# Cross-attention stage: normalising and quantising moved to GpSimd, two fp32 products split into three products of rounded parts, the residual added in the output buffer

## The reference

```python
x2 = (x - mean(x)) / sqrt(var(x) + 1e-5)
q = (x2 @ Wq + bq) / sqrt(32)                  # per head
q = round(q / s) * s                           # s = max|q| / 127, per token and head
attn = softmax(q @ k.T)                        # k, v quantised ahead of this stage
attn = round(attn / a) * a                     # a = max(attn) / 255, per row
x = x + (attn @ v) @ Wp + bp
```

## Time and profile before

| what | value |
|---|---|
| time, median of 3 runs | 3387.66 us (3382.36 to 3388.56) |
| time of the profiled execution | 3388.41 us |
| its span, first to last instruction | 3386.2 us |
| mean granted TensorE clock | 0.978 |
| this stage, from its first VectorE instruction to the start of the last `add` | 1911.38 to 2209.21 us |

### The profile page before, as it was taken

The page is one execution under the profiler, slowest core; times in us unless marked ns, Lnnn a source line. Parts: engine busy times, 40 slices in busy tenths (PEclk is TensorE's granted clock), DMA queues, the critical chain, the costliest instruction groups (busy, mean ns, idle before and its releaser), DMA issues. The chain is left out here.

```text
span 3386.2 us, 59964 instructions
## 1 busy us (share of the span) xinstructions
PE 3173.4 (94%) x18834; PEld 2548.5 (75%) x18834; DVE 2200.1 (65%) x4849; ACT 1902.5 (56%) x4657; POOL 1666.0 (49%) x3107
## 2 busy tenths in 40 slices
PE   6799999999999999999989888879998999998998
PEld 3688888888888888888878555568876777777543
DVE  5577777777777677777753388865548576685432
ACT  3677777777767777777631177743436464463111
POOL 2777787777787777778630000035553002011322
PEclk8899999999999999999989899999999999999999
DMA  4222222222222222222353323433334222221853
GB/s 113 65 73 70 53 74 66 69 73 63 61 69 72 70 63 73 69 59 70 85 175 99 128 106 143 152 110 119 99 112 150 81 66 73 83 75 66 263 101 54
DMA packets 432407, 310.46 MB, mean 92 GB/s; under 512 B 130496, under 2 KB 347456, under 8 KB 431072
## 3 DMA queue, kind: packets, MB, share of 16 engines
q1 hardware_dynamic: 423792, 289.57, 28.9%
q0 software_dynamic: 8432, 18.88, 2.8%
HBM read 177.97 MB, written 130.43 MB: 91 GB/s over the span
## 5 line engine op out<-in xcount | busy, mean ns | idle before, releaser
L631 PE MATMUL gd_PJ<-xn_lead,gd_w_rest 128*128 128x512 f32 x1024 | 420.8, 411 | 0.5 <-DVE gd_w_rest L786 0.5
L631 PE MATMUL gd_PJ<-xn_lead,gd_w_lead 128*128 128x512 f32 x1024 | 402.4, 393 | 0.0
L631 PE MATMUL gd_PJ<-xn_rest,gd_w_lead 128*128 128x512 f32 x1024 | 401.2, 392 | 0.0
L1079 POOL TENSOR_TENSOR gd_prod<-gd_L,gd_T 32x14 f32<-32x14 f32 (+6 forms) x896 | 323.3, 361 | 70.5
L1082 POOL TENSOR_TENSOR gd_T<-gd_T,gd_prod 32x14 f32<-32x14 f32 (+6 forms) x896 | 313.4, 350 | 71.7 <-POOL gd_prod L1079 2.7
L793 DVE SCALAR_TENSOR_TENSOR gd_conv<-gd_pre,gd_cur_a,gd_conv 128x512 f32<-128x512 f32 x384 | 301.8, 786 | 12.8 <-ACT gd_conv L958 2.4
L631 PEld LDWEIGHTS gd_PJ<-xn_lead,gd_w_lead 128*128 128x128 f32 x1024 | 193.2, 189 | 43.4
L631 PEld LDWEIGHTS gd_PJ<-xn_lead,gd_w_rest 128*128 128x128 f32 x1024 | 194.0, 189 | 38.4 <-DVE gd_w_rest L786 0.9
L631 PEld LDWEIGHTS gd_PJ<-xn_rest,gd_w_lead 128*128 128x128 f32 x1024 | 194.4, 190 | 35.2
L932 DVE SCALAR_TENSOR_TENSOR gd_og<-gd_B,ptab,gd_gate 128x512 f32<-128x512 f32 x64 | 48.0, 751 | 243.6 <-PE gd_B L645 243.6
L640 PE MATMUL gd_B<-gd_W,gd_Lo 128*128 128x64 f32 (+1 forms) x1536 | 174.6, 257 | 23.8 <-DMA gd_T<-inverse_image 14.7
(11 more groups left out here) (476 smaller groups left out, 8744.3 us busy)
## 6 DMA issues: line engine op xcount, KB each, us to landing
expert_rows<-xt_blank SPq DMA_DIRECT2D x16, 2112.0 KB, 7.3
turned_queries_keys<-f_wq SPq DMA_DIRECT2D x16, 1280.0 KB, 6.0
x_wo<-decay_sums SPq DMA_DIRECT2D x64, 256.0 KB, 3.8
triangles<-gd_Lo SPq DMA_DIRECT2D x64, 256.0 KB, 3.5
gd_W<-turned_image SPq DMA_DIRECT2D x64, 256.0 KB
gd_T<-inverse_image SPq DMA_DIRECT2D x64, 256.0 KB
gated_outputs<-gd_og SPq DMA_DIRECT2D x64, 256.0 KB, 2.8
go_ogt<-gated_outputs SPq DMA_DIRECT2D x16, 1024.0 KB, 5.9
```

Source lines behind the costliest of these rows:

```text
L631: mm = pe.matmul(bank, w_parts[wp][:, j, k, :], rhs, start=(k == 0 and wp == 1), stop=(k == KT - 1 and wp + xp == 0))
L1079: nc.gpsimd.tensor_tensor(prod[:, rows, 0:j], L16[:, rows, j:j + 1].to_broadcast(shape), T16[:, j:j + 1, 0:j].to_broadcast(shape), ALU.mul ...
```

## The change

- `queries` and `project` use operands of two rounded parts each (a lead in the 32-bit rounded matmul type, and the rest, value minus lead). Each k-tile takes three matmuls, rest x lead, lead x rest and lead x lead, in place of one fp32 product. ScalarE's copies `copy_xT` and `copy_oT` write the lead, and two new VectorE steps, `rest_x` and `rest_o`, subtract it from PSUM.
- At the start of the stage `wq` (its buffer now lies in `E`) is split by ScalarE (lead) and VectorE (rest), k-tile by k-tile; `wp` is split by GpSimd before it clears `blank`.
- `normalise` for tiles 3 and on moves to GpSimd as two instructions with a broadcast column, and `quantise` for tiles 2 and on as four. VectorE keeps the scale and its reciprocal (`inverse_scale`, now right after `biased`) and copies the scale at the end of the slot (`keep_scale`). Tiles 0 to 2 and 0 to 1 stay on VectorE.
- `fetch` writes the residual plus bias into `y` itself, after it has waited for the store of that buffer; `add` no longer waits for the store.

```diff
-            def fetch(t, par):
-                nc.gpsimd.tensor_tensor(xt[:, par, :], xres[:, bass.ds(t, 1), :]..., bpb[:, :], ALU.add).then_inc(bias_ready, 1)
+            def fetch(t, half, par):
+                pool.wait_ge(out_done[par], half * 16 + 16)
+                nc.gpsimd.tensor_tensor(y[:, par, :], xres[:, bass.ds(t, 1), :]..., bpb[:, :], ALU.add).then_inc(bias_ready, 1)
+            def normalise(t):
+                pool.wait_ge(x_turned, t)
+                nc.gpsimd.tensor_copy(st[:, 0:1], mean[:, bass.ds(t, 1)]).then_inc(st_ready, 1)
+                nc.gpsimd.tensor_copy(st[:, 1:2], rstd[:, bass.ds(t, 1)]).then_inc(st_ready, 1)
+                pool.wait_ge(st_ready, (t - 2) * 2)
+                nc.gpsimd.tensor_tensor(xn[:, :], xres[...], st[:, 0:1].to_broadcast([P, DIM]), ALU.subtract).then_inc(xc_ready, 1)
+                pool.wait_ge(xc_ready, t - 2)
+                nc.gpsimd.tensor_tensor(xn[:, :], xn[:, :], st[:, 1:2].to_broadcast([P, DIM]), ALU.mult).then_inc(xn_ready, 1)
+            def quantise(t):
+                pool.wait_ge(qr_ready, t + 1)
+                nc.gpsimd.tensor_tensor(qf[:], qf[:], bc(qr[:, :], XD), ALU.mult).then_inc(qn_ready, 1)
...
+                nc.gpsimd.tensor_tensor(qf[:], qf[:], scale[...].to_broadcast([P, XH, XD]), ALU.mult).then_inc(qn_ready, 1)
...
+                nc.gpsimd.tensor_tensor(qf[:], qf[:], magic[...].to_broadcast([P, XH, XD]), ALU.add).then_inc(qn_ready, 1)
...
+                nc.gpsimd.tensor_tensor(qi[:, :], qf[...], magic[:, 0:1].to_broadcast([P, DIM]), ALU.subtract).then_inc(qi_ready, 1)
             def slot(t, i, s, left):                       # GpSimd
+                if left > 2:
+                    normalise(t + 3)
+                if left > 1:
+                    quantise(t + 2)
                 if left > 0:
                     pool.wait_ge(y_ready, t + 1)
-                    fetch(t + 1, 1 - s)
+                    fetch(t + 1, i + s, 1 - s)
+            for g in range(GR):                            # GpSimd, ahead of the blank
+                nc.gpsimd.tensor_copy(wp_parts[0][:, g, :], wp[:, g, :]).then_inc(wp_led, 1)
+                pool.wait_ge(wp_led, g + 1)
+                nc.gpsimd.tensor_tensor(wp_parts[1][:, g, :], wp[:, g, :], wp_parts[0][:, g, :].bitcast(F32), ALU.subtract).then_inc(wp_split, 1)
                 for k in ks:                               # TensorE, queries; project alike
-                    mm = pe.matmul(psQ[:, :], xT[:, k, :], wq[:, k, :], ...)
+                    for xp, part in ((1, 0), (0, 1), (0, 0)):
+                        mm = pe.matmul(psQ[:, :], xT[xp][:, k, :], wq_parts[part][:, k, :], ...)
             def slot(t, i, s, left):                       # VectorE
                 integers(t, 0)
+                if left > 1:
+                    rest_x(t + 2)
                 maxima(t, s, 2)
...
                 if left > 1:
                     biased(t + 2)
+                    inverse_scale(t + 2)
                 integers(t, 2)
+                if prev:
+                    rest_o(t - 1)
                 if left > 0:
                     maxima(t + 1, 1 - s, 0)
                 copy_p(t, 2)
-                if left > 2:
-                    normalise(t + 3)
...
                 if left > 1:
-                    quantise(t + 2, s)
+                    keep_scale(s)
                 if prev:
-                    add(t - 1, i - 1 + s, 1 - s)
+                    add(t - 1, 1 - s)
+            for k in range(KT):                            # VectorE, start of the stage, after normalise(1)
+                dve.wait_ge(wq_led, k + 1)
+                nc.vector.tensor_tensor(wq_parts[1][:, k, :], wq[:, k, :], wq_parts[0][:, k, :].bitcast(F32), ALU.subtract).then_inc(wq_split, 1)
+                if k == 0:
+                    rest_x(0)
+            rest_x(1)
```

More of the change, by code:

```diff
@@ L1448, in cross_tiles @@
         o = sb("o", [P, XH, XD])
-        oT = sb("oT", [P, GR, P])
+        oT = [sb(n, [P, GR, P], F32R) for n in ("oT_lead", "oT_rest")]
         y = sb("y", [P, 2, DIM])
+        magic, scale = sb("magic", [P, 1]), sb("scale", [P, 1])
         blank = sb("blank", [P, ROW])
@@ new lines, in quantise @@
+            def quantise(t):
+                pool.wait_ge(qr_ready, t + 1)
+                nc.gpsimd.tensor_tensor(qf[:], qf[:], bc(qr[:, :], XD), ALU.mult).then_inc(qn_ready, 1)
+                pool.wait_ge(qn_ready, (t - 2) * 3 + 1)
+                nc.gpsimd.tensor_tensor(qf[:], qf[:], scale[:, 0:1].unsqueeze(2).to_broadcast([P, XH, XD]), ALU.mult).then_inc(qn_ready, 1)
+                pool.wait_ge(qn_ready, (t - 2) * 3 + 2)
+                nc.gpsimd.tensor_tensor(qf[:], qf[:], magic[:, 0:1].unsqueeze(2).to_broadcast([P, XH, XD]), ALU.add).then_inc(qn_ready, 1)
+                pool.wait_ge(qn_ready, (t - 2) * 3 + 3)
+                nc.gpsimd.tensor_tensor(qi[:, :], qf[:].rearrange("p h d -> p (h d)"), magic[:, 0:1].to_broadcast([P, DIM]), ALU.subtract).then_inc(qi_ready, 1)
@@ L1534, in queries @@
                 for k in ks:
-                    mm = pe.matmul(psQ[:, :], xT[:, k, :], wq[:, k, :], start=(k == 0), stop=(k == KT - 1))
+                    for xp, part in ((1, 0), (0, 1), (0, 0)):
+                        mm = pe.matmul(psQ[:, :], xT[xp][:, k, :], wq_parts[part][:, k, :],
+                                       start=(k == 0 and xp == 1), stop=(k == KT - 1 and xp + part == 0))
                 if ks[-1] == KT - 1:
@@ L1577, in project @@
                     pe.wait_ge(oT_ready, t + 1)
+                    if isinstance(t, int) and t == 0:
+                        pe.wait_ge(wp_split, GR)
                 for g in gs:
-                    mm = pe.matmul(psQ[:, :], oT[:, g, :], wp[:, g, :], start=(g == 0), stop=(g == GR - 1))
+                    for op, part in ((1, 0), (0, 1), (0, 0)):
+                        mm = pe.matmul(psQ[:, :], oT[op][:, g, :], wp_parts[part][:, g, :],
+                                       start=(g == 0 and op == 1), stop=(g == GR - 1 and op + part == 0))
                 if gs[-1] == GR - 1:
@@ L1795, in _ @@
             normalise(1)
+            for k in range(KT):
+                dve.wait_ge(wq_led, k + 1)
+                nc.vector.tensor_tensor(wq_parts[1][:, k, :], wq[:, k, :], wq_parts[0][:, k, :].bitcast(F32), ALU.subtract).then_inc(wq_split, 1)
+                if k == 0:
+                    rest_x(0)
+            rest_x(1)
             biased(0)
-            quantise(0, 0)
+            inverse_scale(0)
+            keep_scale(0)
+            quantise(0)
             biased(1)
+            inverse_scale(1)
+            keep_scale(1)
             normalise(2)
-            quantise(1, 1)
+            quantise(1)
             maxima(0, 0, 0)
@@ L1804, in _ @@
             outputs(TILES - 1)
-            add(TILES - 1, TILES // 2 - 1, 1)
+            rest_o(TILES - 1)
+            add(TILES - 1, 1)
 DH = 128
```

67 lines of the change are left out of this document (45 added, 22 removed).

## The result

The changed kernel takes 3392.81 us (median of 16 runs, 3385.49 to 3398.14), the kernel before, run beside it, 3384.38 (16 runs, 3382.06 to 3391.31): a ratio of 1.0019 [1.0013, 1.0026]. The medians are 8.4 us apart, the ratio stands for 6.4. The forecast was +8.3. The profiled execution has a span of 3390.7 us against 3386.2 and a mean granted clock of 0.979 against 0.978.

The account below looks back on a forecast made before the run. VectorE, in its written order, was taken to set the slot, TensorE a close second. Thirteen slots at +0.4 us (+5.2) and the start (+3.1) gave +8.3: 3396 us, forecast's own range 3389 to 3403, wider range 3379 to 3407.

Parts of the forecast that it names:

- The holds: VectorE instructions standing still behind GpSimd's SBUF reads: nine exposed starts a slot, 1.45 us, 1.1 after waits.
- A slot, part by part: Steady slot of 16.89 us between two `add`s: -0.7 without conflicts, +1.1 from conflicts, +0.4 us in sum.
- The moves: Normalising and quantising leave VectorE: 2.38 us busy and 0.15 waiting less per slot; `keep_scale` adds 0.17.
- The query split: Query product in rounded parts: `rest_x` adds 0.68 us to VectorE per slot, its query wait shrinks by 0.15.
- The output split: Output product in rounded parts: `rest_o` adds 0.68 us to VectorE per slot, the wait before `copy_p(t, 2)` 0.45.
- The late output product: `project` starts about 1.5 us later behind `rest_o`; the 0.26 us wait before `copy_p(t, 2)` grows by 0.45.
- the granted clock in the stage falls below 1.0: One of the listed signs that the prediction is wrong, for the stage's clock; no size given.
- The start: Start of the stage: splitting `wq` and `rest_x` delay the first rounding of `E` by 3.1 us, bounds +2.2 and +4.5.
- The end: Last tile: `rest_o` adds 0.7 us, its product is 0.7 shorter, so nothing.
- The moved residual: `fetch` writing into `y` moves the wait for the store from VectorE to GpSimd; nothing on either side.
- GpSimd's durations: GpSimd's six broadcast products over 128x512 take 1.04 us each, 1.04 to 1.3 in the changed profile.
- No `turn_q` waited for GpSimd: GpSimd's quantising latency was claimed covered by some 5 us; `turn_q` waiting for GpSimd would show the prediction wrong.

Follow-up runs that it names:

- changed_light: The changed kernel with one of two normalising and three of four quantising GpSimd instructions left out; 3386.84 us, ratio 1.0019 to the kernel before.
- nb_reduced: The changed kernel with the constant of `nb` added by a reduction over pairs instead of a `tensor_scalar`; 3394.05 us, ratio 1.0024 to the kernel before.
- moves_light: The changed kernel with both products in fp32, and one of two normalising and three of four quantising GpSimd instructions left out; 3374.38 us, ratio 0.9969.
- queries_nb: The changed kernel with the output product in fp32, no `rest_o`, and the constant of `nb` added by a reduction over pairs; 3365.01 us, ratio 0.9957.
- rest_o_first: The changed kernel with `rest_o` ahead of `integers(t, 2)` on VectorE instead of behind it; 3390.67 us, ratio 1.0011 to the kernel before.
- split_only: The changed kernel with normalising and quantising back on VectorE for all tiles, split products kept; 3428.34 us, ratio 1.0121 to the kernel before.
- moves_only: The changed kernel with both products in fp32 again, the moves to GpSimd kept; 3377.56 us, ratio 0.9971 to the kernel before.
- queries_split: The changed kernel with the output product in fp32 and no `rest_o`, the query product still split; 3372.94 us, ratio 0.9967 to the kernel before.

## Why the prediction was right in its total, and where its terms were not

The total and the sign held (+6.4 for +8.3 us), and so did the mechanism in outline: relief on VectorE given back by holds and by the split of the output product. That the total came so close is luck in part, for errors of several steps cancel. By its steps:

- *The holds.* Forecast 1.45 us a slot raw; measured 1.3 on the mean of fifteen slots and 1.5 in the steady ones. The shapes exposed and not exposed are the forecast ones. The price taken, 1.1 after a quarter lost in waits, is where it erred: a hold has no fixed price. In the changed kernel halving them earned nothing (changed_light; in nb_reduced the clock fell as well), and beside a busy TensorE neither (moves_light). One kind of hold cost its whole length in queries_nb. The step took each start for a draw; the trace shows the last rounding held in the same place in slot after slot.
- *A slot, part by part.* Twelve slots give means. The moves: forecast -2.53 of work and handshake, +0.17 for `keep_scale` (it takes 0.11, and its spacing in the timeline is 0.02) and +1.1 of holds, -1.3; measured -0.82 (16.05 for 16.87), since TensorE with fp32 products is the next bound 0.8 below (moves_light, with far fewer holds, has the same slots). The query split: forecast +0.68 - 0.15 = +0.5; measured -0.10 (15.95), since `rest_x` falls into VectorE's waits, which go from 15.2 to 5.6 us in the stretch, and the product is shorter. The output split: forecast +0.68 + 0.45 = +1.1; measured +1.17 (17.11 for 15.95), right in size, but by the last rounding that now meets GpSimd's fourth instruction and not its third. The sum, +0.4 forecast and +0.24 measured, came out because two errors of half a microsecond cancel.
- *The late output product.* The wait of 0.84 was forecast as 0.6 to 0.8. Its price of 0.45 a slot is not shown: in rest_o_first the wait is gone and the stretch to the last rounding is the same 5.6 us. The step did not see that TensorE's 1.9 to 2.1 us of idle time in each slot could cost its clock; "the granted clock in the stage falls below 1.0" was named only as a way to be wrong. It fell once in the steady slots of the profiled execution (that slot took 17.47, where its place in the alternation gives 16.5, about 0.1 us on the mean slot) and much more in split_only and nb_reduced. `rest_o_first` shows that order alone does not cure the slot: the wait went, and holds took its place.
- *The start* was put at +3.1 at the first rounding and is +1.0, and +0.3 at the first `add`. The splits of `wq` came as laid out, with the first one held:

```profile
1911.85 1.72 DVE L1863 TENSOR_TENSOR xt_wq_rest<-xt_E,xt_wq_lead 128x512 fp32r<-128x512 f32 x1
...
1914.31 0.77 PE L1572 MATMUL xt_Q<-xt_wq_lead,xt_xT_rest 128*128 128x512 f32 x1 [3.25 <-DVE xt_xT_rest L1760]
...
1918.29 0.60 PE L1572 MATMUL xt_Q<-xt_wq_lead,xt_xT_rest 128*128 128x512 f32 x1
...
1921.06 0.68 DVE L1772 TENSOR_TENSOR xt_qf<-xt_Q,x_bqb 128x512 f32<-128x512 f32 x1
```

  From the stage's first instruction the product starts 1.5 us later than before (forecast 2.2) and `biased(0)` 1.9 later (3.2); the second product and what follows gave back 0.9 more. I had summed each delay as if the work behind it kept its distance. So 2.8 us of the 3.1 never reached the first `add`; that error and the next one, of 2.4 us, cancel.
- *The end* was put at nothing and is +2.4. In the last product the pace falls to the low level; the last `add` waits for it:

```profile
2208.52 0.39 PE L1620 MATMUL xt_Q<-xt_wp_lead,xt_oT_lead 128*128 128x512 f32 x1
...
2209.50 0.63 PE L1620 MATMUL xt_Q<-xt_wp_lead,xt_oT_lead 128*128 128x512 f32 x1
2209.92 0.63 PE L1620 MATMUL xt_Q<-xt_wp_lead,xt_oT_rest 128*128 128x512 f32 x1
...
2212.59 0.69 DVE L1820 TENSOR_TENSOR xt_y<-xt_Q,xt_y 128x512 f32<-128x512 f32 x1 [4.76 <-PE xt_Q L1620]
```

  The last slot took 9.71 us (8.07 before). It is not the split alone: moves_only, with an fp32 product, had 9.76 there, moves_light 8.06.
- *The moved residual* was to cost nothing, and VectorE and GpSimd show no wait for it that anything stands behind: GpSimd waits for the store (5.4 us in a slot) and is done in time.
- *GpSimd's durations* were 1.04 as forecast, but 1.36 for the product with a value for each head. No `turn_q` waited for GpSimd.

What stays open: why `fetch` starts by turns some 0.2 us earlier and later; how often the clock falls, since each kernel has one profiled execution; and why exactly the tail lost its clock in some kernels. That changed_light's missing gain lies in waits for TensorE is read from sums in two traces, not shown by an experiment that fixes TensorE's pace. That the last rounding's place sets the price of the output split is read from the timelines of all the runs; none moves that rounding alone.

## What to carry to other kernels

Price a slot with the second engine in view: work taken from the bound helps only down to where the other engine stands, work added inside its waits is free, and work that the other engine must wait for costs twice, itself and the idle time it opens. When a change splits a product into rounded parts, ask where the extra subtraction stands in the written order; the query product took it for nothing, the output product paid 0.4 to 0.5% for it. Before removing a conflict between VectorE and GpSimd, find out which held instruction ends last and on which GpSimd instruction it ends: work saved ahead of such a place is waited out there. With 13.5 us of VectorE's waits in ten slots halving the holds earned nothing; with 5.6 removing one kind of hold won its length, in one profiled execution.

## What the runs showed of the hardware

- A `tensor_scalar` on 128x4 fp32 in SBUF (170 ns) took up to 1.31 us beside GpSimd; a `tensor_reduce` over pairs with the same result never took more than 164 ns, though 9 of 64 (nb_reduced) and 6 of 64 (queries_nb) started inside a GpSimd instruction. This fits the Trainium skill ("SBUF — State Buffer", Who interferes with whom): only 2-port modes and instructions with two SBUF inputs exclude GpSimd.
- On GpSimd a product of 128x512 with a column broadcast along the row took 1.04 us, with 16 values broadcast over 32 elements each 1.36, with a full second operand 1.27 to 1.30.
- Idle stretches of 1.9 to 2.0 us a slot before the output product, with 9.2 us of other waits in the stretch, came with a granted clock of 0.89 (split_only); six extra bf16 matmuls ahead of the product brought it to 0.97 and the kernel 15 us forward (+25.6 us over the kernel before in place of +40.7). Stretches of 1.9 to 2.1 us in the changed kernel came with 0.99.
- A rounding of 128x1024 that started inside a GpSimd instruction of 128x512 in the last rounding's place ended 0.55 us behind it, in every slot (changed kernel, rest_o_first, queries_split).
